# A four-layer decoder on one Trainium2 core: where the slots' zeros are kept, the order of the norm's spreads, an early trial maximum on GpSimd, and one block for convolution and token layouts

## The chip, the cores and the metric

The kernel runs on one core of one Trainium2 chip. The metric is the device time of one execution in microseconds (us); lower is better. Inside the core TensorE (PE; its weight loads are listed as PEld), VectorE (DVE), ScalarE (ACT), GpSimd (POOL) and SyncE (SP) each run their own list of instructions and meet only at semaphores. DMAs here are issued by SP or POOL.

## What is computed

Eight sequences of 256 tokens with 128 features (2048 tokens, held feature by token) pass through four layers, each with self attention, cross attention and a feed-forward part, and each part adds its output to the residual. Every part begins with the first function below; the parts that the change touches inside are the second (layer 1's attention: convolution, SiLU, unit-length heads) and the third (layer 2's feed-forward: the activations are rounded by one scale taken over the whole tensor).

```python
def _layernorm(x, axis=-1, eps=1e-05):
    m = jnp.mean(x, axis=axis, keepdims=True)
    v = jnp.var(x, axis=axis, keepdims=True)
    return (x - m) / jnp.sqrt(v + eps)

# layer 1, attention
q = _causal_depthwise_conv_silu(hidden_states @ q_w, conv_q_w)   # 4 taps; k and v alike
beta = jax.nn.sigmoid(hidden_states @ b_w)
q = _l2norm(q)        # per head of 16 features; k alike
...                   # a delta rule over chunks of 32 tokens
# layer 2, feed-forward
def _act_fake_quant(x, clip_factor):
    scale = jax.nn.sigmoid(clip_factor) * jnp.max(jnp.abs(x)) / QMAX
    return jnp.clip(_ste_round(x / scale), -QMAX - 1.0, QMAX) * scale
```

## The kernel before

The program is a row of blocks. A block gives each engine its own list; at its end all engines meet at a barrier, and the next block's first instructions come after it. `loads_done` is a block of its own, in which only SP waits for a DMA's semaphore, so it holds back everything written after it. Within a block each engine runs its list in the order in which it is written; nothing is reordered.

**The start.** `start_loads` issues the input, the small weights, the context and the masks. `clear_buffers` fills 2560 words of a part of `tiles` (`c.T`, four tiles of 2048 words) with zeros on POOL and has SP copy them to the DRAM buffer `slots_in`, which the experts of layer 0 use later; the zeros lie in tiles 2 and 3. `layer0_attention` issues its weights (`pack_load`), waits with `loads_done` for that copy, and calls `norm_stage`, whose output `n2` is tile 3.

**`norm_stage`** works on 4 chunks of 512 tokens, or 8 parts of 256. PE subtracts the mean (line 270) and sums squares (277), ACT takes squares and roots (398, 407), DVE inverts the roots of two chunks at a time (337). PE then spreads the inverses over the partitions, four parts per inverse (`spreads`, line 290), and DVE multiplies (346). Where `jobs` are handed on, PE multiplies each chunk by the next weights (`follow`, line 314), and ACT or DVE takes the product away. The PE list reads

```python
            spreads(0)
            follow(0)
            spreads(1)
            for i in range(1, NC):
                follow(i)
```

Eight calls have jobs: one with one (the output of layer 2's attention), four with two, two with three and one with four. In the other calls `follow` does nothing.

**Layer 1's convolution and token layouts** are two blocks. `conv_stage` has DVE convolve k, v and q (one multiply and three multiply-adds of 2048 words each, lines 2142 and 2144), ACT apply SiLU in eleven pieces that also permute the tokens (2162) and square k and q (2166), and PE form the gate logits (2131). `delta_tokens` then has PE sum the squares per head (2192, 32 matmuls of 8 columns with the squares as weights), ACT take roots (2207), PE transpose k and v to token rows (2201, eight groups of four), and ACT and DVE copy the groups by turns (2211, 2236). `delta_solve` follows, beginning with PE transposes of the copied keys (2298) that ACT copies.

**Layer 2's feed-forward** (`layer2_mlp`): after the norm, DVE takes the largest magnitude per partition (3450), POOL the largest over the partitions (`partition_all_reduce`, 3421), DVE derives the scale (3453) and rounds (3457, 3458), ACT shifts (3398), PE multiplies (3359). In PE's list 16 products of weights (`join`, 3339) stand ahead of the first of these.

Of the kernel before, what the change touches and what calls it, by code (L numbers as in the profile page):

```python
# [14 lines left out]
P = 128  # L15
# [192 lines left out]
def norm_stage(c, src, dst, eps, centre=True, gain=None, shift=None, times=None, grow=1.0, before=None, add=None,  # L208
# [49 lines left out]
    with nc.Block() as block:  # L258
        @block.tensor
        def _(pe):  # L260
# [64 lines left out]
            follow(0)  # L325
            spreads(1)
            for i in range(1, NC):
                follow(i)
# [669 lines left out]
def clear_buffers(c):  # L998
# [3 lines left out]
    zeros = c.T[:, 2:4, :].rearrange("p a x -> p (a x)")[:, 0:words]  # L1002
# [29 lines left out]
def layer0_attention(c):  # L1032
# [5 lines left out]
    n2 = c.T[:, 3, :]  # L1038
    loads_done(c, c.slots_cleared)
    norm_stage(c, c.X, n2, "eps55", grow=1.0 + 1e-5, also=(c.HN, "eps5"))  # L1040
# [1065 lines left out]
def conv_stage(c, tensors, taps):  # L2106

    nc = c.nc
    a = Arena(c)
    acc = [a.take(N) for _ in tensors]  # L2110
    squares = a.take(2, N)
    ps_g = c.psum[:, 7, 0:2 * P].rearrange("p (n e) -> p n e", e=16)

    def blocks(x):
        return x.rearrange("p (g j t r s) -> p g j t r s", j=4, t=2, r=4, s=32)

    def moves(j):
        if j == 0:
            return [(0, 0, 4)]
        if j == 2:  # L2120
            return [(0, 2, 2), (2, 0, 2)]
        return [(r, r ^ j, 1) for r in range(4)]

    with nc.Block() as block:
        @block.tensor
        def _(pe):
            for n in range(NT):
                b, t = n // 2, n % 2
                for r in range(4):
                    lo = b * S + t * P + 32 * (r ^ (b % 4))  # L2130
                    mm = nc.tensor.matmul(ps_g[32 * r:32 * r + 32, n, :], c.HN[:, lo:lo + 32], c.w("L1a_gates"),
                                          start=True, stop=True, tile_position=(0, 32 * r))
            mm.then_inc(c.gate_logits.sem, 1)

        @block.vector
        def _(dve):
            chain = Chain(dve, c.vector_chain)
            for x, w, y in zip(tensors, taps, acc):
                K = w.shape[1]
                xs = x.rearrange("p (b s) -> p b s", s=S)  # L2140
                ys = y.rearrange("p (b s) -> p b s", s=S)
                chain.link(nc.vector.tensor_scalar(y, x, w[:, K - 1:K], None, ALU.mult))
                for back in range(1, K):
                    ins = nc.vector.scalar_tensor_tensor(ys[:, :, back:], xs[:, :, 0:S - back],
                                                         w[:, K - 1 - back:K - back], ys[:, :, back:],
                                                         ALU.mult, ALU.add)
                    if back < K - 1:
                        chain.link(ins)
                ins.then_inc(c.convolved.sem, 1)
            dve.wait_ge(c.convolved.sem, c.convolved.at(len(tensors)))  # L2150
            chain.clear()

        @block.scalar
        def _(act):
            for n, (x, y) in enumerate(zip(tensors, acc)):
                act.wait_ge(c.convolved.sem, c.convolved.at(n + 1))
                for j in range(4):
                    for lo, at, count in moves(j):
                        w = slice(0, 32 * count)
                        src = blocks(y)[:, :, j, :, lo:lo + count, :].rearrange("p g t r s -> p g t (r s)")  # L2160
                        dst = blocks(x)[:, :, j, :, at:at + count, :].rearrange("p g t r s -> p g t (r s)")
                        ins = nc.scalar.activation(dst[:, :, :, w], src[:, :, :, w], ACT.Silu)
# [2259 lines left out]
```

## Time and profile before

| | |
|---|---|
| time, median of 3 runs | 2698.5 us (2695.79 to 2700.4) |
| the profiled execution's own time | 2686.84 us |
| its span | 2685.0 us |
| busy: PE, DVE, ACT, POOL | 72%, 65%, 43%, 27% |
| instructions | 35915 |

A timeline row gives start, duration, engine, line, operation, output<-input, and in brackets how long the engine stood idle before it and what ended that. Rows of PE merge instructions of one kind; a float32 matmul stands as two instructions in the trace (x64 for 32 matmuls), while a float32 transpose stands as one. A slice of the page is 67 us long.

### The profile page before, as it was taken

The numbers are of one execution on the slowest core, as the hardware profiler recorded it, in microseconds if no ns is written. First come the engines' busy times: TensorE is split into PE (matmuls) and PEld (weight loads), VectorE is DVE, ScalarE is ACT, GpSimd is POOL, SyncE is SP. The second block draws the span as 40 slices with busy tenths as digits, with TensorE's granted clock in tenths as the row PEclk, the third lists the DMA queues.
The fourth block names the chain that finished last, engine by engine and source line by source line (L and its number), as shares of the span: only waits on it lengthen the run. The fifth ranks groups of instructions, "written<-read, shape, count | busy, mean of one in ns | idle before, by whom it ended". The sixth has DMA issues, their size and how long they took to land. (4 is left out here: it accounts for less than half of the span.)

```text
span 2685.0 us, 35915 instructions
## 1 busy us (share of the span) xinstructions
PE 1923.9 (72%) x11203; PEld 1116.0 (42%) x11215; DVE 1756.1 (65%) x5569; ACT 1148.4 (43%) x3148; POOL 716.3 (27%) x638
## 2 busy tenths in 40 slices
PE   5996878843877999979986875556555555556777
PEld 1644436422444666644352543333333333324243
DVE  4235322248766666647746567999999999964554
ACT  3553332141314666641233554555555455542312
POOL 1200050405333333310032411333333333331130
PEclk7988889965988999979988887566666566666878
DMA  4000001220000000000100000000000000000000
GB/s 183 2 1 0 25 19 35 47 110 1 2 2 1 1 1 0 0 0 0 77 14 1 1 1 0 1 1 1 1 1 1 0 1 1 1 1 0 0 0 16
DMA packets 10065, 37.04 MB, mean 14 GB/s; under 512 B 1755, under 2 KB 7008, under 8 KB 8752
## 3 DMA queue, kind: packets, MB, share of 16 engines
q1 hardware_dynamic: 7856, 31.69, 3.0%
q0 software_dynamic: 2048, 3.38, 0.6%
q8 instruction: 80, 1.31, 0.2%
q14 instruction: 81, 0.66, 0.1%
HBM read 30.11 MB, written 5.77 MB: 13 GB/s over the span
## 5 line engine op out<-in xcount | busy, mean ns | idle before, releaser
L3552 PE MATMUL psum<-work 32*128 32x256 f32 x512 | 129.9, 652 | 296.8 <-ACT work L3647 296.8
L3699 DVE MATCH_REPLACE8 work<-work 128x256 f32<-128x256 f32 x768 | 306.4, 414 | 0.0
L3747 POOL TENSOR_TENSOR work<-work 128x1024 f32<-128x1024 f32 x64 | 150.7, 2355 | 509.0 <-ACT work L3647 509.0
L3696 DVE MAX8 work<-work 128x8 f32<-128x256 f32 x768 | 267.8, 415 | 0.0
L3552 PEld LDWEIGHTS psum<-work 32*128 32x128 f32 x512 | 77.3, 309 | 323.1 <-ACT work L3647 165.1
L676 POOL TENSOR_TENSOR work<-work 128x256 f32<-128x256 f32 (+2 forms) x144 | 133.3, 944 | 259.3 <-DVE work L936 259.3
L866 ACT ACTIVATE work<-work 128x128 f32<-128x128 f32 (+1 forms) x320 | 144.9, 454 | 38.0 <-PE psum L736 24.6
L337 DVE RECIPROCAL work<-work 128x256 f32<-128x256 f32 x36 | 62.8, 1749 | 123.2 <-ACT work L407 123.0
L3647 ACT ACTIVATE work<-work 128x256 f32<-128x256 f32 x256 | 128.2, 501 | 0.0
L3575 PE MATMUL psum<-work,tiles 128*8 128x256 f32 x512 | 117.0, 610 | 13.8 <-ACT work L3656 13.8
L3749 POOL TENSOR_TENSOR work<-work 128x1024 f32<-128x1024 f32 x64 | 121.1, 1892 | 6.2 <-DVE work L3721 1.2
L3598 PE MATMUL psum<-small_weights,work 128*128 128x128 f32 x512 | 102.7, 367 | 21.6 <-POOL work L3749 21.6
L3645 ACT ACTIVATE work<-psum,work 128x256 f32<-128x256 f32 x256 | 117.5, 459 | 0.0
L3598 PEld LDWEIGHTS psum<-small_weights,work 128*128 128x128 f32 x512 | 84.3, 194 | 70.1 <-POOL work L3749 52.6
L3699 DVE MATCH_REPLACE8 work<-work,psum 128x256 f32<-128x256 f32 x256 | 103.4, 420 | 0.0
L905 DVE CUSTOM_DVE_ANT_0 work<-psum,work 128x128 f32<-128x128 f32 (+1 forms) x320 | 99.6, 368 | 2.8
L3696 DVE MAX8 work<-psum 128x8 f32<-128x256 f32 x256 | 90.9, 421 | 7.2 <-PE psum L3552 5.8
L2080 DVE TENSOR_TENSOR work<-work,psum 128x320 f32<-128x320 f32 (+1 forms) x56 | 32.1, 574 | 88.4 <-PE psum L1951 88.4
L832 ACT ACTIVATE work<-psum,big_weights 128x256 f32<-128x256 f32 x128 | 57.8, 474 | 73.2 <-PE psum L722 72.8
L796 PE MATMUL psum<-work 128*64 128x256 f32 (+2 forms) x640 | 72.7, 346 | 19.6 <-DVE work L931 19.6
L736 PE MATMUL psum<-small_weights,work 128*128 128x128 f32 x512 | 83.5, 281 | 3.7 <-POOL work L676 3.7
L270 PE MATMUL psum<-residual,small_weights 128*128 128x512 f32 x96 | 58.5, 741 | 38.7 <-PEq L189 22.8
(597 smaller groups left out, 4682.0 us busy)
## 6 DMA issues: line engine op xcount, KB each, us to landing
big_weights<-L0f_dram SPq DMA_DIRECT2D x1, 6053.5 KB, 25.8
big_weights<-L_dram SPq DMA_DIRECT2D x1, 5892.0 KB, 16.6
big_weights<-L_dram SPq DMA_DIRECT2D x1, 4952.5 KB, 15.7
big_weights<-L_dram SPq DMA_DIRECT2D x1, 2091.0 KB, 20.2
big_weights<-L_dram SPq DMA_DIRECT2D x1, 1630.5 KB, 11.8
big_weights<-L0f_dram SPq DMA_DIRECT2D x1, 1630.5 KB, 6.4
slots_in<-tiles SPq DMA_DIRECT2D x1, 1280.0 KB, 9.4
residual<-x_dram SPq DMA_DIRECT2D x1, 1024.0 KB, 4.9
```

The lines of the kernel that those rows point to most:

```text
L676: ins = nc.gpsimd.tensor_tensor(part, part, rsum[:, g % 4, q:U:U // n].unsqueeze(2) .broadcast_to([P, n, seen(q)]), ALU.mult)
L866: ins = nc.scalar.activation(probs[:, g % 2, u, 0:seen(u)], src, ACT.Exp, bias=nbias[:, g % 2, u:u + 1], scale=scale, accum_out=sums[:, g ...
L905: ins = nc.vector.tensor_tensor_reduce(raw[:, s, u, 0:seen(u)], scores(g)[:, u, 0:seen(u)], mask(mb, u % 2)[:, 0:seen(u)], 1.0, NEG, ALU.a ...
L3552: mm = nc.tensor.matmul(scores(n)[:, u, :], qb[head, tile % 2, u % 2 * P:(u % 2 + 1) * P], kb[head, tile % 2, :], start=True, stop=True, t ...
L3575: mm = nc.tensor.matmul(held(tile)[at:at + D, :], values[:, 2 * b + kt, lo:lo + D], turned[:, n % 2, head, kt, :], start=(kt == 0), stop=( ...
L3598: mm = nc.tensor.transpose(bank(4 + head)[:, at:at + P], probs[:, n % 2, 2 * head + q, kt * P:(kt + 1) * P], ident)
L3645: nc.scalar.activation(probs[:, s, u, :], scores(n)[:, u, :], ACT.Exp, bias=nbias[:, s, u:u + 1], scale=SCALE)
L3647: ins = nc.scalar.activation(rest[:, s, u, :], raw[:, s, u, :], ACT.Exp, bias=nbias[:, s, u:u + 1], scale=SCALE)
L3696: ch.step(v.max(top8[:, n % 2, u, r, :], src[:, u, :]))
L3699: ins = v.match_replace(raw[:, n % 2, u, :], top8[:, n % 2, u, r, :], src[:, u, :], REPLACED)
L3747: ch.link(g.tensor_tensor(mine, mine, rest[:, n % 2], ALU.subtract))
L3749: g.tensor_tensor(mine, mine, rsum[:, n % 2, :].unsqueeze(2).broadcast_to([P, U, S]), ALU.mult) \
```

## The change

Four edits.

1. The zeros are kept in tiles 1 and 2, and the block that waits for their copy to DRAM stands behind the first norm instead of ahead of it.
2. In every norm the second half's spreads stand ahead of the first chunk's handed-on products.
3. `conv_stage` and `delta_tokens` become one block, `conv_tokens`. The order is q, k, v; the head sums of q are made after its squares, those of k after its squares; ACT copies six groups and DVE two; ACT loads its function tables five times rather than three.
4. In the norm ahead of layer 2's feed-forward POOL makes a `partition_all_reduce` of a zeroed word.

```diff
@@ norm_stage
             powers(1)
             spreads(0)
-            follow(0)
             spreads(1)
-            for i in range(1, NC):
+            for i in range(NC):
                 follow(i)
@@ clear_buffers
-    zeros = c.T[:, 2:4, :].rearrange("p a x -> p (a x)")[:, 0:words]
+    zeros = c.T[:, 1:3, :].rearrange("p a x -> p (a x)")[:, 0:words]
@@ layer0_attention
     n2 = c.T[:, 3, :]
+    norm_stage(c, c.X, n2, "eps55", grow=1.0 + 1e-5, also=(c.HN, "eps5"))
     loads_done(c, c.slots_cleared)
-    norm_stage(c, c.X, n2, "eps55", grow=1.0 + 1e-5, also=(c.HN, "eps5"))
     loads_done(c, c.big_loaded)
@@ conv_tokens, in place of conv_stage and delta_tokens: PE's list
...
+            mm.then_inc(c.gate_logits.sem, 1)
+            add_heads(0, ps_q)
+            pe.wait_ge(c.permuted.sem, c.permuted.at(2))
+            for n in range(4):
+                turn(n)
+            pe.wait_ge(c.gates_shifted.sem, c.gates_shifted.at(1))
+            add_heads(1, ps_k)
+            pe.wait_ge(c.permuted.sem, c.permuted.at(3))
+            for n in range(4, 8):
+                turn(n)
@@ DVE's list
+            convolve(0)
+            dve.wait_ge(c.gate_logits.sem, c.gate_logits.at(1))
+            chain.link(vec.tensor_tensor(gates, ps_g, mix_b, ALU.add))
+            vec.tensor_tensor(gates, gates, mix_bias, ALU.add).then_inc(c.gates_shifted.sem, 1)
+            convolve(1)
+            convolve(2)
+            dve.wait_ge(c.rooted.sem, c.rooted.at(1))
+            chain.link(vec.reciprocal(inv, lengths))
...
+            for n in by_vector:
+                _, dst, t, b0 = groups[n]
+                dve.wait_ge(c.tokens_turned.sem, c.tokens_turned.at(n + 1))
+                vec.tensor_copy(dst[:, t, b0:b0 + 4, :], bank(n)).then_inc(c.tokens_kept_v.sem, 1)
@@ ACT's list
+            soften(0)
+            square(0)
+            act.wait_ge(c.gates_shifted.sem, c.gates_shifted.at(1))
+            nc.scalar.activation(gates, gates, ACT.Sigmoid).then_inc(c.gates_ready.sem, 1)
+            nc.scalar.activation(warm, c.w("one"), ACT.Silu)
+            soften(1)
+            square(1)
+            for n in range(4):
+                keep(n)
+            act.wait_ge(c.lengths_ready.sem, c.lengths_ready.at(2))
+            nc.scalar.activation(lengths[:, P:2 * P], c.psum[:, 6, 0:P], ACT.Sqrt, bias=c.w("eps12"))
+            nc.scalar.activation(lengths[:, 0:P], c.psum[:, 7, 2 * P:3 * P], ACT.Sqrt, bias=c.w("eps12")) \
+                .then_inc(c.rooted.sem, 1)
+            nc.scalar.activation(warm, c.w("one"), ACT.Silu)
+            soften(2)
+            for n in (4, 6):
+                keep(n)
@@ layer2_mlp
-    norm_stage(c, c.X, c.HN, "eps5")
+    a = Arena(c)
+    a.off = 2 * N
+    trial = a.take(2)
+
+    def first_reduction(pool):
+        nc.gpsimd.memset(trial, 0.0).then_inc(c.zeros_made.sem, 1)
+        pool.wait_ge(c.zeros_made.sem, c.zeros_made.at(1))
+        nc.gpsimd.partition_all_reduce(trial[:, 1:2], trial[:, 0:1], P, bass.bass_isa.ReduceOp.max)
+
+    norm_stage(c, c.X, c.HN, "eps5", beside=(("gpsimd", first_reduction),))
```

`by_vector` is (5, 7); `soften` is the SiLU of one tensor, `square` its squares, `keep` the copy of one group, `turn` a group's four transposes, `add_heads` 16 head sums.

The first place is PE's list at layer 1's norm and what follows it. Before (290 is `spreads`, 314 `follow`, 2131 the gate logits, 2192 the head sums, 2201 the transposes):

```order
L290 MATMUL psum<-work,small_weights 128x256 x4
L314 MATMUL psum<-normed_input,big_weights 128x512 x3
L290 MATMUL psum<-work,small_weights 128x256 x4
L314 MATMUL psum<-normed_input,big_weights 128x512 x9
L258 UNCONDITIONAL_BRANCH
L2125 UNCONDITIONAL_BRANCH
L2131 MATMUL psum<-big_weights,normed_input 32x16 x64
L2124 UNCONDITIONAL_BRANCH
L2187 UNCONDITIONAL_BRANCH
L2192 MATMUL psum<-big_weights,work 128x8 x32
L2201 MATMUL psum<-small_weights,tiles 128x128 x32
```

And now, with the same steps at lines 290, 2773, 2756 and 2766:

```order
L290 MATMUL psum<-work,small_weights 128x256 x8
L314 MATMUL psum<-normed_input,big_weights 128x512 x12
L258 UNCONDITIONAL_BRANCH
L2750 UNCONDITIONAL_BRANCH
L2773 MATMUL psum<-big_weights,normed_input 32x16 x64
L2756 MATMUL psum<-big_weights,work 128x8 x16
L2766 MATMUL psum<-small_weights,tiles 128x128 x16
L2756 MATMUL psum<-big_weights,work 128x8 x16
L2766 MATMUL psum<-small_weights,tiles 128x128 x16
```

The four late spreads moved ahead of the first three products, the block boundary between logits and head sums is gone, and each half of the head sums stands ahead of half of the transposes.

The second place is ACT's list after k's SiLU in the joined block (2835 SiLU, 2840 squares, 2845 copies, 2857 and 2858 roots, 2860 a one-word SiLU, with the semaphore that a row waits for in brackets):

```order
L2840 ACTIVATE work<-tiles 128x2048 [waits permuted]
L2845 COPY work<-psum 128x512 [waits tokens_turned] x4
L2857 ACT_TABLE_LOAD
L2857 ACTIVATE work<-psum,small_weights 128x128 [waits lengths_ready]
L2858 ACTIVATE work<-psum,small_weights 128x128
L2860 ACT_TABLE_LOAD
L2860 ACTIVATE work<-small_weights 128x1
L2835 ACTIVATE tiles<-work 128x2x256 [waits convolved]
```

Before, all three SiLUs and both squares stood ahead of the first root; now v's SiLU stands behind the roots, which wait for the head sums.

The third place is POOL's list at layer 2's feed-forward, first before (3419 clears a buffer, the row without operands at 3421 belongs to the reduction behind it):

```order
L449 UNCONDITIONAL_BRANCH
L3417 UNCONDITIONAL_BRANCH
L3419 MEMSET work 128x768
L3421 ISA
L3421 ISA work<-work 128x1
L3427 COPY work<-big_weights 128x8x4
```

and now (3331 and 3333 are the trial in the norm's block, 3443 and 3445 the old steps):

```order
L3331 MEMSET work 128x2
L3333 ISA
L3333 ISA work<-work 128x1
L258 UNCONDITIONAL_BRANCH
L3441 UNCONDITIONAL_BRANCH
L3443 MEMSET work 128x768
L3445 ISA work<-work 128x1
L3451 COPY work<-big_weights 128x8x4
```

The row without operands moved with the first reduction into the norm's block; the real reduction has none of its own any more.

## Rows read from the trace of the kernel before

**Rows 1.** Page, part 2: TensorE's granted clock in 40 slices, tenths of full.

```profile
PEclk7988889965988999979988887566666566666878
```

**Rows 2.** Waits of SP's queue, 0 to 40 us: total, times, longest.

```profile
SPq L189 <- DMA slots_in<-tiles: 6.3, 1, 6.3
```

**Rows 3.** Timeline, 0 to 75 us: start, duration, engine, line, operation.

```profile
8.13 0.64 SPq L174 DMA_DIRECT2D big_weights<-L0f_dram  x1
...
15.83 4.34 PE L270 MATMUL psum<-residual,small_weights 128*128 128x512 f32 x6 [15.83 <-PEq L189]
...
31.20 2.81 DVE L352 SCALAR_TENSOR_TENSOR normed_input<-normed_input,psum 128x256 f32<-128x256 f32 x8
...
34.70 0.23 DVE L1231 COPY work<-big_weights 128x128 f32<-128x128 f32 x1 [0.69 <-PEq L189]
```

**Rows 4.** DMA issues, 0 to 40 us: KB, us from issue to landing.

```profile
big_weights<-L_dram SPq DMA_DIRECT2D x1, 1630.5 KB, 11.8
slots_in<-tiles SPq DMA_DIRECT2D x1, 1280.0 KB, 9.4
```

**Rows 5.** Line 290 in eight windows, one per late spread: length, PE busy, clock.

```profile
554.30:555.30 1.00, 0.91 (x8) 0.74 0.00 0
...
sum 8.30, PE 7.59; mean PE 0.95
```

**Rows 6.** Line 346 (DVE): what its engine sat idle for, us, times.

```profile
  PE psum L290: 37.7, 8
```

**Rows 7.** Timeline, layer 1's norm.

```profile
547.74 1.75 DVE L337 RECIPROCAL work<-work 128x256 f32<-128x256 f32 x1 [0.58 <-ACT work L407]
...
550.14 4.28 PE L314 MATMUL psum<-normed_input,big_weights 128*128 128x512 f32 x6 [1.22 <-DVE normed_input L346]
```

**Rows 8.** Timeline, layer 1's convolution and token layouts.

```profile
565.46 7.08 DVE L2144 SCALAR_TENSOR_TENSOR work<-tiles,big_weights,work 128x2040 f32<-128x2040 f32 x3
...
572.57 2.84 ACT L2162 ACTIVATE tiles<-work 128x512 f32<-128x512 f32 x11 [7.19 <-DVE work L2144]
...
591.92 3.69 ACT L2166 ACTIVATE work<-tiles 128x2048 f32<-128x2048 f32 x2
...
595.91 13.79 PE L2192 MATMUL psum<-big_weights,work 128*128 128x8 f32 x64 [30.52 <-PEq L2124]
...
611.29 1.28 ACT L2214 ACT_TABLE_LOAD   x1
612.58 0.42 ACT L2214 ACTIVATE work<-work 128x256 f32<-128x256 f32 x1
...
613.95 2.48 DVE L2236 COPY work<-psum 128x512 f32<-128x512 f32 x4
...
616.75 2.04 PE L2298 MATMUL psum<-small_weights,work 128*128 128x128 f32 x16 [1.40 <-PEq L2186]
```

**Rows 9.** Windows: length, PE, PEld, DVE, ACT, POOL busy, clock.

```profile
577.00:595.90 18.90, 0.00 (x0) 0.02 (x1) 12.01 (x6) 9.30 (x25) 0.00 (x0) 0.50 0.00 0
595.90:609.50 13.60, 13.59 (x64) 13.60 (x65) 0.85 (x2) 1.25 (x1) 0.00 (x0) 0.50 0.00 1
609.50:612.50 3.00, 3.00 (x15) 3.00 (x16) 1.75 (x1) 2.27 (x3) 0.00 (x0) 0.50 0.00 0
613.00:620.00 7.00, 5.30 (x46) 4.86 (x45) 4.58 (x9) 3.70 (x7) 0.39 (x1) 1.00 0.00 1
```

**Rows 10.** Timeline, layer 2's feed-forward.

```profile
1580.73 2.29 DVE L3450 TENSOR_REDUCE work<-normed_input 128x1 f32<-128x2048 f32 x1 [0.32 <-PEq L258]
...
1581.94 5.56 PE L3339 MATMUL psum<-big_weights 128*128 128x128 f32 x32
...
1587.24 0.38 POOL L3421 PARTITION_ALL_REDUCE work<-work  x1 [5.81 <-issue]
...
1587.65 0.16 DVE L3453 TENSOR_TENSOR work<-work,big_weights 128x1 f32<-128x1 f32 x1 [4.64 <-POOL work L3421]
...
1590.33 0.38 PE L3359 MATMUL psum<-work 128*128 128x512 bf16 x1 [2.83 <-ACT work L3398]
```

More of the change, by code:

```diff
@@ L2102, in layer0_experts @@
         s.advance(n)
[L2106 to L2162, printed above, removed]
-                ins.then_inc(c.permuted.sem, 1)
-            for n, x in enumerate((tensors[0], tensors[2])):
-                act.wait_ge(c.permuted.sem, c.permuted.at((1, 3)[n]))
-                nc.scalar.activation(squares[:, n, :], x, ACT.Square)
-    c.gate_logits.advance(1)
-    c.convolved.advance(len(tensors))
-    c.permuted.advance(len(tensors))
-    return squares
@@ L2865, in layer1_attention @@
     norm_stage(c, c.X, c.HN, "eps5", jobs=[(c.w(f"L1a_w{s}"), None, None, t, None) for s, t in zip("qkv", (q, k, v))])
-    squares = conv_stage(c, [k, v, q], [c.w(f"L1a_conv_{s}") for s in "kvq"])
     def words(lo, *dims):
@@ L2891, in layer1_attention @@
     probs = [c.T[:, 3, 0:12 * P].rearrange("p (j a x) -> p j a x", a=3, x=P), words(at, 4, 3, P)]
-    delta_tokens(c, k, v, squares, kt, vt, gates, lengths, inv, sizes)
+    conv_tokens(c, q, k, v, [c.w(f"L1a_conv_{s}") for s in "qkv"], kt, vt, gates, lengths, inv, sizes)
     delta_solve(c, kt, vt, sizes, sizes_r, k_r, X, tri, pair, own)
@@ L3311, in layer2_mlp @@
     loads_done(c, c.loaded_ahead)
-    norm_stage(c, c.X, c.HN, "eps5")
+    a = Arena(c)
+    a.off = 2 * N
[5 more added lines that the diff above has]
+    norm_stage(c, c.X, c.HN, "eps5", beside=(("gpsimd", first_reduction),))
+    c.zeros_made.advance(1)
     a = Arena(c)
```

159 lines of the change are left out of this document (96 added, 63 removed).

## The prediction

> **What bounds the kernel now.** I first read the page's clock line: TensorE is granted full clock only in part, down to 5 and 6 tenths in the second half [rows 1]. No engine is busy all the time, so a local edit is worth what it takes off the wait that ends last at its place. I therefore went from the waits to the timeline of four places. At the start everything stands behind the copy of zeros to DRAM: SP waits 6.3 us for it [rows 2]. In the norms with handed-on products DVE idles 37.7 us in 8 places for late spreads [rows 6], which themselves hold PE for 7.6 us [rows 5]. In layer 1, PE does nothing from 577 to 595.9 and then 13.8 us of head sums while ACT and DVE wait [rows 8, 9]. In layer 2's feed-forward a reduction that takes 0.4 us starts at 1587.2, though its input is there at 1583.0 [rows 10].
>
> **The start: 6.3 us.** SP has issued the big weights at 8.77 (8.13 + 0.64); the first norm starts at 15.83 [rows 3], because the copy of the zeros lands at 5.97 + 9.4 = 15.4, where 5.97 is its issue [rows 4]. Now the norm starts at about 9.2. It ends 6.3 earlier, at 27.7 instead of 34.0 (31.20 + 2.81) [rows 3]. What is late next: the zeros' copy is down at 15.4, and layer 0's weights, issued just ahead of 8.13, at about 19.6 (11.8 after issue) [rows 4]. Both lie under the norm, so nothing takes the wait's place. The DMA of zeros has the same size and is read from tiles that the norm doesn't write. The bounds are close: 6.0 if one barrier more stands in the way, 6.6 if the whole stretch from 8.77 to 15.4 goes.
>
> **The spreads: 7.0 us.** In eight norms four spreads stand between the first chunk's products and the rest. They take 0.95 us on average, 7.6 in total [rows 5], and behind them PE runs products one after another to the end of the stage, so time taken from there counts. DVE's idle 37.7 us is not the gain: DVE is off the path once its four parts are early, and PE still has the same products. What comes back is a delay at the new place. In layer 1's norm the second reciprocal ends at 549.49 and the first product starts at 550.14 [rows 7]; 0.9 us of spreads now stand in between, so it starts about 0.3 late, and that stage gains 0.6. Four norms are like this, by 0.1 to 0.5. In the other four the first product waits for a further step on ACT or POOL, or for another bank, and the spreads hide. Small gaps around the old place, and one wait for a later chunk, go too (0.6 us, my estimate). So 7.6 - 1.2 + 0.6 = 7.0. The upper bound is 8.5 (no collision and every gap gone). The lower bound is zero: should each early set delay the first product by its whole length, PE has only exchanged the two; below zero is excluded, since the products and their number stay.
>
> **Convolution and layouts: 12.9 us.** All in times of the old trace. DVE is through with the first tensor at 572.5, and each further one takes 8.3 (565.46 + 7.08; ACT's last SiLU starts at 591.92 - 2.84 = 589.1, two tensors later) [rows 8]. New path:
> - SiLU of q 572.6 to 575.4, squares (half of 3.69) to 577.3, 16 head sums on PE: half of 13.79 is 6.9, to 584.2. PE has been idle till then and its clock is at 0.50 [rows 9].
> - DVE adds 0.85 for the gates [rows 9] and is through with k at 581.7. SiLU of k to 584.6, squares to 586.5. Between them on ACT lie the sigmoid and two table loads (0.42 + 2 x 1.28 and a word, 3.2 us), hidden in its wait from 577.3 to 581.7.
> - PE turns k's four groups from 584.6: 15 transposes took 3.0 us at 0.50 [rows 9], so 16 take 3.4, to 588.0. Then k's head sums: 6.9 at that level, to 594.9, or 3.45 at twice the clock, to 591.5.
> - ACT copies four groups meanwhile and loads the root's table under its wait. Queued behind the wait for the head sums on ACT is everything for v: two short roots 0.6 (from 0.42 for a sigmoid of twice the width), table load 1.28 and one word 0.2, SiLU of v 2.84. That is 4.9 us, to 599.8 or 596.4; v itself has been convolved since 590.0. PE's last transposes wait for it: 3.4, one copy on DVE 0.62 (2.48 for four) and hand-overs 0.2; the block's end costs 0.3 (616.43 to 616.75) [rows 8].
>
> So the keys' transposes of the next block start at 604.3 or 600.9 instead of 616.75: 12.4 or 15.8 earlier. There the old trace had clock 1.00 from 613.0 on [rows 9] and 16 transposes in 2.04 [rows 8]. After 5 us without work on PE they may now run at 0.50, 3.4 us, which costs up to 1.4. Bounds: 11.0 and 15.8. I take 12.9, nearer to the low end, as the only row for head sums is at 0.50.
>
> Which end it is hangs on what lifts the clock. The rows show 13.6 us of unbroken head sums at 0.50, and 1.00 from 613.0 on, 3.5 us after the transposes began [rows 9]. That speaks for the transposes lifting it, and with them the second head sums. The Trainium skill (TensorE: Matmul & The Clock Gate, Part 4: PE-mode transpose) says that transposes don't count as PE being busy in the way matmuls do. By that rule k's head sums would stay at 1.2 GHz; the trace leans against it.
>
> One more table load (ACT, behind the roots) is on the path, at 1.28: in the old trace the sigmoid starts 0.01 us after its load ends [rows 8]. The Trainium skill (ScalarE: Activation LUTs, What ACT_TABLE_LOAD costs) states 2.66 us for a switch, drain included. By that the sum would be 1.4 less, an estimate from the page; the trace shows no such drain, and I keep 1.28.
>
> **The trial maximum: 2.8 us.** The old reduction starts 5.8 us after the clearing of a buffer, "issue" being all that it waits for [rows 10], and its row without operands now stands in the norm's block. That block lasts some 10 us on PE and DVE with POOL empty, so 5.8 + 0.4 + a small clearing hide there. The real one can start when DVE's maximum is there (1580.73 + 2.29 = 1583.0), so DVE goes on at 1583.5 instead of 1587.65: 4.1 earlier. But PE has 16 weight products ahead of the first product of the activations, until 1581.94 + 5.56 = 1587.5, and that first product started at 1590.33 [rows 10]. Once ACT's part is 4 us early, PE's own list is late next: 1590.33 - 1587.5 = 2.8. Upper bound 4.1, lower bound 0 (the 5.8 us belong to each block anew).
>
> **Sum.** 6.3 + 7.0 + 12.9 + 2.8 = 29.0. The profiled execution, 2686.84, would become 2657.8. The median of the runs is 11.7 higher, 2698.5; the gain is the same in us, so 2669.5.
>
> **Rivals.**
> - The second head sums stay at 1.2 GHz, and so does the start of the next block. 11.0 instead of 12.9, rounded with the rest: 2671.4. For it: 13.6 us at 0.50 in the only rows of such work. Against: the rise after the transposes.
> - The early spreads cost at the new place what they did at the old. Then 22.0 remain: 2676.5. For it: in four norms DVE's first two parts take only 0.65 us. Against: that covers most of 0.9, and in the other four a further step follows.
> - Upper ends everywhere: 6.6 + 8.5 + 15.8 + 4.1 = 35.0, so 2663.5. For it the clock's rise behind the transposes; against it PE's 16 products.
> - The trial doesn't do what it says: the reduction in the next block waits anew. 26.2 remain: 2672.3. Against it: the second reduction of the old block has no such row ahead of it.
> - Slower: layer 0's experts, slices 5 to 8 of the page, some 230 us at 8 to 9 tenths of the clock [rows 1] with PE the busy engine. They now begin some 8 us earlier against the start. Should the clock stay at the lower level there for t us more than before, it costs t/2; from 58 us on that eats the 29 us, and with 70 the time is 2704.5. Against it: the list there is unchanged, and the clock falls where PE stands idle.
> - Nothing of it arrives, as the stages hide one another: within 0.2% of 2698.5. Against it: barriers at every block.
>
> **How the numbers follow.** Forecast 50%, the second head sums at 1.2 GHz 20, spreads without gain 10, upper ends 10, trial in vain 5, slower 3, nothing 2. So faster 95, same 2, slower 3; "same" is within 0.2% (5.4 us), what a measurement of this kernel can tell from no change. The lower bounds together, 6.0 + 0 + 11.0 + 0 = 17.0, give 2681.5, the upper ones 2663.5. With some 2 us of spread between medians I give 2661 to 2682.
>
> **What would show it.** The first norm's matmuls start at about 9.2. Line 346 no longer waits for line 290, and products follow without a break. The head sums are in two runs of about 6.9 and 3.5 to 6.9 us; Layer 1 begins some 8.5 us earlier (6.3 and the norms before it), so v's SiLU starts at 585 to 589 and the next block's transposes of keys at 592 to 596. The reduction starts within 0.2 us of DVE's maximum. It is wrong if the clock at layer 1's head sums is at another level than both cases, if another DMA ends the start, or if an expert stage changes its length by more than 3 us.

## Result and the profile after

| | before | after |
|---|---|---|
| time, median of 4 runs, us | 2699.24 (2695.79 to 2700.4) | 2662.49 (2659.91 to 2665.62) |
| the profiled execution's own time | 2686.84 | 2659.91 |
| its span | 2685.0 | 2658.1 |
| ratio | | 0.9866 [0.9849, 0.9884] |

36.8 us less, where 29.0 were forecast; 2662.5 lies in the given range, near its lower end. The profiled executions are only 26.9 us apart. I cut both spans at the first root of each of the 18 norms (the one-word root on ACT with which a norm begins):

| stretch (between first roots) | before | after | gain |
|---|---|---|---|
| up to the first norm | 17.09 | 10.64 | 6.5 |
| layer 0 up to its experts | 290.0 | 289.5 | 0.6 |
| layer 0's experts | 232.6 | 242.3 | -9.7 |
| layer 1's first norm and attention | 293.0 | 278.4 | 14.6 |
| the rest of layer 1 | 499.1 | 499.5 | -0.5 |
| layer 2's attention | 89.2 | 85.2 | 4.0 |
| norms and cross attention of layer 2 | 150.0 | 145.4 | 4.6 |
| layer 2's feed-forward | 54.6 | 51.8 | 2.8 |
| the rest | 1059.4 | 1055.3 | 4.1 |

TensorE's granted clock on the page, for [rows 1]: it is low in the same parts.

```profile
PEclk7988889875988999989997896566666566667878
```

Each edit shows at its place. The start, in after's timeline, and the next stage behind the norm, for [rows 3]:

```profile
9.38 4.78 PE L270 MATMUL psum<-residual,small_weights 128*128 128x512 f32 x6 [9.38 <-PEq L170]
...
25.18 2.80 DVE L351 SCALAR_TENSOR_TENSOR normed_input<-normed_input,psum 128x256 f32<-128x256 f32 x8
29.06 0.23 DVE L1230 COPY work<-big_weights 128x128 f32<-128x128 f32 x1 [1.07 <-PEq L189]
```

The norm begins 6.45 earlier (15.83 in [rows 3]), and SP's wait of [rows 2] is gone. The boundary behind the norm takes 1.07 instead of 0.69: the block that waits for the zeros' copy stands there now. The next stage's first copy on DVE starts at 29.06 instead of 34.70, only 5.6 earlier: 0.4 went to that boundary and 0.4 to the norm's first centring products, which took 4.78 instead of 4.34.

The norms: what DVE's multiplication (line 345, formerly 346) and PE's handed-on products (314) cost and wait for in the whole program (busy us, mean ns, then the idle time ahead of them). First before, then after.

```profile
L314 PE MATMUL psum<-normed_input,big_weights 128*128 128x512 f32 x96 | 50.9, 676 | 8.5 <-ACT normed_input L412 4.4 <-DVE normed_input L346 4.1
L290 PE MATMUL psum<-work,small_weights 32*128 32x256 f32 x288 | 42.2, 462 | 15.1 <-DVE work L337 9.6 <-ACT normed_input L403 5.2
L314 PE MATMUL psum<-tiles,big_weights 128*128 128x512 f32 x48 | 29.4, 767 | 6.3 <-POOL tiles L458 2.6 <-ACT tiles L412 2.3 <-DVE tiles L346 1.5
```

```profile
L314 PE MATMUL psum<-normed_input,big_weights 128*128 128x512 f32 x96 | 50.4, 681 | 0.7 <-ACT normed_input L411 0.7
L290 PE MATMUL psum<-work,small_weights 32*128 32x256 f32 x288 | 46.2, 484 | 18.7 <-DVE work L336 13.2 <-ACT normed_input L402 5.3
L314 PE MATMUL psum<-tiles,big_weights 128*128 128x512 f32 x48 | 27.6, 741 | 0.8 <-POOL tiles L457 0.8
...
L345 DVE SCALAR_TENSOR_TENSOR normed_input<-normed_input,psum 128x256 f32<-128x256 f32 x120 | 40.2, 406 | 0.1
```

DVE's 37.7 us of waiting for spreads [rows 6] are gone. PE stood 8.5 + 6.3 = 14.8 us ahead of its products before, and 1.5 after; the spreads wait 18.7 us instead of 15.1. Where these 14.8 us lie decides what they mean. The timeline of before has 14.5 of them ahead of the very first product of the eight norms (2.57, 2.07, 1.22, 1.50, 2.26, 1.98, 1.22 and 1.64), and 0.34 in one place behind it. One such norm, of layer 2, before and then after:

```profile
1443.58 0.71 PE L290 MATMUL psum<-work,small_weights 32*128 32x256 f32 x8 [1.47 <-DVE work L337]
1446.55 3.78 PE L314 MATMUL psum<-tiles,big_weights 128*128 128x512 f32 x4 [2.26 <-ACT tiles L412]
1450.26 1.24 PE L290 MATMUL psum<-work,small_weights 32*128 32x256 f32 x8
1451.43 5.94 PE L314 MATMUL psum<-tiles,big_weights 128*128 128x512 f32 x12
```

```profile
1427.62 1.24 PE L290 MATMUL psum<-work,small_weights 32*128 32x256 f32 x8 [0.59 <-DVE work L336]
1429.39 1.50 PE L290 MATMUL psum<-work,small_weights 32*128 32x256 f32 x8 [0.54 <-DVE work L336]
1430.82 8.34 PE L314 MATMUL psum<-tiles,big_weights 128*128 128x512 f32 x16
```

The first product comes 3.20 us after the first spreads instead of 2.97, so the filled wait itself brings nothing; the gain lies between the first and the last product. Over the eight norms the first products come 2.2 us later behind the first spreads, and the stretch from first to last product is 9.7 us shorter (90.7 to 81.0).

Layer 1's convolution and layouts in after's timeline, for [rows 8]:

```profile
578.95 6.99 PE L2756 MATMUL psum<-big_weights,work 128*128 128x8 f32 x32 [12.01 <-ACT work L2840]
...
586.11 3.67 PE L2766 MATMUL psum<-small_weights,tiles 128*128 128x128 f32 x16 [0.17 <-ACT tiles L2835]
...
589.58 3.93 PE L2756 MATMUL psum<-big_weights,work 128*128 128x8 f32 x32
...
593.82 0.36 ACT L2858 ACTIVATE work<-psum,small_weights 128x128 f32<-128x128 f32 x1
594.19 1.28 ACT L2860 ACT_TABLE_LOAD   x1
...
595.49 0.20 ACT L2860 ACTIVATE work<-small_weights 128x1 f32<-128x1 f32 x1
595.60 2.82 ACT L2835 ACTIVATE tiles<-work 128x512 f32<-128x512 f32 x11
...
603.20 3.65 PE L2160 MATMUL psum<-small_weights,work 128*128 128x128 f32 x16 [1.05 <-PEq L2749]
```

From DVE's first step of the convolution (564.13 before, 565.68 after) to the next block's transposes (616.75 before [rows 8]) 52.6 us passed, now 37.5. Those transposes take 3.65 us instead of 2.04.

The feed-forward of layer 2 in after's timeline, for [rows 10]: first the trial, then the real maximum.

```profile
1555.46 0.38 POOL L3333 PARTITION_ALL_REDUCE work<-work  x1 [5.69 <-issue]
...
1560.68 2.29 DVE L3474 TENSOR_REDUCE work<-normed_input 128x1 f32<-128x2048 f32 x1 [0.32 <-PEq L258]
...
1561.89 5.95 PE L3363 MATMUL psum<-big_weights 128*128 128x128 f32 x32
...
1563.07 0.35 POOL L3445 PARTITION_ALL_REDUCE work<-work  x1 [1.69 <-DVE work L3474]
...
1567.89 0.38 PE L3383 MATMUL psum<-work 128*128 128x512 bf16 x1
```

The trial takes the 5.7 us of "issue", the real reduction starts 0.1 us behind the end of DVE's maximum, and PE goes over to the activations when its products of weights end at 1567.8.

What doesn't fit are the experts. In after's trace ACT and DVE stand still there for 25.7 and 27.0 us, as in no row of the first trace of before ("remote" is the name that the profile gives to what ended the wait):

```profile
514.87 0.60 ACT L1980 ACTIVATE work<-psum 128x512 f32<-128x512 f32 x1 [25.72 <-remote]
```

```profile
517.72 1.42 DVE L2079 TENSOR_TENSOR work<-work,psum 128x512 f32<-128x512 f32 x2 [26.98 <-remote]
```

### The profile page after: what moved, and what is told of

Its sections match the earlier page's. It is cut to its first block and busy times, and to the rows that moved or that the text cites. A ratio compares the mean times of both kernels' runs of the same rounds, so it can differ in the third digit from the quotient of the medians.

```text
span 2658.1 us, 35910 instructions
## 1 busy us (share of the span) xinstructions
PE 1915.9 (72%) x11203; PEld 1113.3 (42%) x11215; DVE 1755.9 (66%) x5567; ACT 1152.6 (43%) x3155; POOL 716.7 (27%) x640
## 5 line engine op out<-in xcount | busy, mean ns | idle before, releaser
L1980 ACT ACTIVATE work<-psum 128x512 f32<-128x512 f32 (+1 forms) x64 | 33.1, 517 | 133.3 <-PE psum L1949 92.0
```

## Experiments

Two theories stood against each other on the missing 10 us (theory A: a stall that comes and goes, whichever kernel runs; theory B: one that the change makes). Beside that each edit was run alone, so that its term of the sum has a measured size. Gains in us are one minus the ratio, times the median of before on that chip. (By the medians alone the four edits give 4.4, 11.0, 14.4 and 4.7 us, all within the intervals below.) Three chips took part beside the first occasion: A (the first four runs, before at 2683.3), B (the next four, 2686.3) and C (the last three, 2697.1).

### Before again (chip A)

No edit.

> The kernel before, unchanged, once more with a profile. The question is the expert stage (its last product of experts to the next norm's first root), which took 9.7 us less in the first profile of before than in the one of after. Theory A (a stall that most executions have): ACT and DVE stand still for about 25 us while GpSimd issues the 32 gathers, PE idles some 20 us, the tail behind the last gather is about 22 us and the stage some 10 us longer than in the first profile; the execution is near the median, 2696 to 2700, and the first profile of before was the exception. Theory B (the change itself makes the stall): no such stall here, the tail behind the gather is 8.4 us again, and the execution is at about 2687 or its extra time lies elsewhere.

2684.53 us, its expert stage 230.4 us, no stall. So this run alone does not back theory A; before itself is 16 us quicker here (2683.3) than on the first occasion (2699.2).

### Each edit alone (chips A and B)

The start:

```diff
-    zeros = c.T[:, 2:4, :].rearrange("p a x -> p (a x)")[:, 0:words]
+    zeros = c.T[:, 1:3, :].rearrange("p a x -> p (a x)")[:, 0:words]
-    loads_done(c, c.slots_cleared)
     norm_stage(c, c.X, n2, "eps55", grow=1.0 + 1e-5, also=(c.HN, "eps5"))
+    loads_done(c, c.slots_cleared)
```

> Only the first edit: the slots' zeros in tiles 1 and 2, and the wait for their copy behind the first norm. By the prediction 6.3 us less than before (ratio 0.9977), the first norm starting at about 10.6 instead of 17.1. Rival: part of it is lost because one more block boundary now stands between the norm and the attention (about 1 us) and since PE meets its first work colder: 5 to 5.6 us in all. If the expert stage's stall hangs on where in time the stage begins, this kernel's expert stage differs from before's by some 10 us in either direction.

Ratio 0.9982 [0.9973, 0.9991]: 4.8 us (2.4 to 7.2). The first root is at 10.51 instead of 16.73, so 6.2 at the place; the expert stage is as in before (231.9). The interval holds the forecast and the rival. The traces speak for less than 6.3: DVE's first copy of the next stage starts at 34.4 to 35.3 in the six traces without this edit and at 28.6 to 29.8 in the six with it as it stands here, 5.8 earlier on average. The added boundary (1.07 instead of 0.69) is 0.4 of what is missing.

The spreads:

```diff
             spreads(0)
-            follow(0)
             spreads(1)
-            for i in range(1, NC):
+            for i in range(NC):
                 follow(i)
```

> Only the second edit: in every norm with handed-on products all eight spreads stand ahead of the products. By the prediction 7.0 us less (ratio 0.9974), between 0 and 8.5. From the traces of before and after the norms and what follows them, clock included, suggest 6 to 12. Rival: the early spreads only swap places with the first products, so under 2 us. In the profile DVE's multiplications have no idle time left for the spreads if the first is right.

Ratio 0.9952 [0.9938, 0.9965]: 12.9 us (9.4 to 16.6), above my upper bound of 8.5. The rows of lines 314 and 290 in this kernel:

```profile
L314 PE MATMUL psum<-normed_input,big_weights 128*128 128x512 f32 x96 | 48.5, 659 | 0.3 <-ACT normed_input L411 0.3
L290 PE MATMUL psum<-work,small_weights 32*128 32x256 f32 x288 | 46.1, 483 | 19.3 <-DVE work L336 13.8 <-ACT normed_input L402 5.2
L314 PE MATMUL psum<-tiles,big_weights 128*128 128x512 f32 x48 | 28.0, 748 | 0.8 <-POOL tiles L457 0.8
```

The wait ahead of the products falls from 14.8 to 1.1, that ahead of the spreads rises by 4.2. As in after, nearly all of what falls stood ahead of the first products, where the early spreads now fill it. So these two sums are no measure of the gain. The eight norms, cut in three, are (before again and before are traces of the kernel before; sums in us; before again and the edit alone ran on one chip):

| stretch | before again | before | after | spreads alone |
|---|---|---|---|---|
| norm's first root to its first spread | 55.2 | 56.6 | 57.0 | 52.9 |
| first spread to first product | 26.3 | 26.2 | 28.4 | 29.4 |
| first to last product | 92.5 | 90.7 | 81.0 | 79.5 |
| together | 173.9 | 173.6 | 166.4 | 161.7 |

Alone, the edit makes the eight norms 12.2 us shorter, near the timed 12.9; in after they are 7.2 shorter than in before. The difference lies mostly in the first row, in the centring ahead of the spreads, which no edit touches, and there the granted clock differs: in one norm of layer 3 it is 0.92 with the edit alone, 0.79 in before and 0.78 in after, and the stretch takes 9.3, 10.9 and 11.0 us. The trace of this kernel is its slowest run, and only 7.8 us shorter than before again: the eight stages that begin with these norms are 14.6 us shorter, but stages without an edit took longer (2.3 us in the experts, 3.7 in the rest of layer 1, 1.3 in layer 2's feed-forward).

The convolution:

```diff
-    squares = conv_stage(c, [k, v, q], [c.w(f"L1a_conv_{s}") for s in "kvq"])
-    delta_tokens(c, k, v, squares, kt, vt, gates, lengths, inv, sizes)
+    conv_tokens(c, q, k, v, [c.w(f"L1a_conv_{s}") for s in "qkv"], kt, vt, gates, lengths, inv, sizes)
```

> Only the third edit: convolution and token layouts in one block. By the prediction 12.9 us less (ratio 0.9952). From the trace of after the sharper value is 15.1 for the block and 1.6 lost in the transposes behind it, so 13.5. Rival: layer 2's attention, which was 4 us shorter in after without an edit of its own but the spreads, owes that to this edit (the clock's level handed on): then 16 to 18.

Ratio 0.9938 [0.9925, 0.9952]: 16.6 us (12.9 to 20.1), where the rival had put it. In its trace layer 1's first norm and attention take 271.2 us against 289.9 in before again. Of these 18.7 us 15.4 are the block (52.7 to 37.3); the other 3.3 come from the rest of the attention, transposes of the next block included, which has no edit and takes 210 to 218 us in the traces with the joined block and 214 to 216 in the others. And layer 2's attention takes 85.2 against 89.2. That 4 us goes with TensorE's clock, 0.92 against 0.88 on the stage's average. PE stands idle ahead of that stage's norm in both; in before again the clock falls to 0.50 in that pause, here it stays at 1.00. The first centring products, and windows with the clock (third number from the end), of before again and of this kernel:

```profile
1328.23 5.46 PE L270 MATMUL psum<-residual,small_weights 128*128 128x512 f32 x6 [3.54 <-PEq L170]
```

```profile
1328.30:1333.60 5.30, 5.30 (x6) 1.75 (x6) 0.00 (x0) 2.58 (x4) 0.00 (x0) 0.50 1.13 427
```

```profile
1312.43 2.81 PE L270 MATMUL psum<-residual,small_weights 128*128 128x512 f32 x6 [3.65 <-PEq L170]
```

```profile
1308.80:1312.40 3.60, 0.00 (x0) 0.00 (x0) 2.05 (x3) 0.00 (x1) 0.00 (x0) 1.00 0.00 0
1313.00:1315.70 2.70, 2.70 (x14) 0.86 (x12) 0.00 (x0) 2.38 (x5) 0.00 (x0) 1.00 0.66 279
```

The six products take 5.46 and 2.81 us. The pauses are 3.54 and 3.65 us long, and the longer one keeps the clock; so it is in all 13 traces, 3.65 in the six that keep it and 3.54 in the seven that lose it, so that the pause's length is not what decides. All traces with the joined block have 85.2 there, but for the kernel with v's SiLU first below (86.9); all without have 89.1 to 89.4. Why the clock falls in the one and not in the other is open.

The trial maximum:

```diff
-    norm_stage(c, c.X, c.HN, "eps5")
+    a = Arena(c)
+    a.off = 2 * N
+    trial = a.take(2)
+    ...
+    norm_stage(c, c.X, c.HN, "eps5", beside=(("gpsimd", first_reduction),))
+    c.zeros_made.advance(1)
```

> Only the fourth edit: the trial maximum on GpSimd in the norm ahead of layer 2's feed-forward. By the prediction 2.8 us less (ratio 0.9990), between 0 and 4.1, with DVE going on 4 us earlier and PE's 16 products of weights late next. Rival: the 5.8 us belong to each block anew, then 0, and the real reduction again starts 4 us behind DVE's maximum. The timed interval will hardly tell 2.8 from 0; the profile's rows will.

Ratio 0.9987 [0.9977, 0.9996]: 3.5 us (1.1 to 6.2). The stage takes 51.5 us instead of 54.3 to 54.6 in the three traces of before, that is 2.9 to 3.1 less. The rival falls: the real reduction has no "issue" ahead of it.

```profile
1580.55 0.35 POOL L3431 PARTITION_ALL_REDUCE work<-work  x1 [1.69 <-DVE work L3460]
```

### After again (chip B)

No edit.

> The kernel after, unchanged, beside before on one chip. The single edits gained 4.4, 11.0 and 14.35 us there; with some 2.8 for the trial maximum the sum is 32.5 (ratio 0.988). Theory A (the stall in the expert stage comes and goes from execution to execution or from chip to chip, in before and after alike): in the profile here the products of layer 0's experts run through while GpSimd issues the gathers, the tail behind the last gather is some 8.5 us, and the gap to before is the sum, about 32. Theory B (all four edits together make the stall): PE again idles some 20 us at the gathers, in this kernel alone, and the gap to before is only some 22.

2643.38 us against 2686.26, ratio 0.9840 [0.9826, 0.9853]: 42.9 us. There is no stall, and the expert stage takes 227.5; theory B falls, though the gap is not theory A's 32 either. But the gap is more than the sum of the single edits, 4.8 + 12.9 + 16.6 + 3.5 = 37.8 (the intervals of these terms would allow it), and 46.2 between the spans of this trace and before again. Of these 46.2, 10.5 lie in stretches that no edit touches, and where the mean clock was higher (0.89 against 0.86, 0.87 against 0.85, 0.92 against 0.88): layer 0's attention 156.6 instead of 160.2, the experts 227.5 instead of 230.4, layer 2's attention 85.2 instead of 89.2. The attention of layer 0, before again and after again:

```profile
17.00:177.00 160.00, 139.49 (x1327) 76.96 (x1326) 63.19 (x131) 83.87 (x99) 23.00 (x13) 0.86 0.10 42
```

```profile
11.00:167.00 156.00, 135.96 (x1327) 75.23 (x1326) 63.19 (x131) 83.59 (x98) 23.24 (x13) 0.89 0.15 60
```

### Head sums ahead of the transposes (chip B)

```diff
             add_heads(0, ps_q)
-            pe.wait_ge(c.permuted.sem, c.permuted.at(2))
-            for n in range(4):
-                turn(n)
             pe.wait_ge(c.gates_shifted.sem, c.gates_shifted.at(1))
             add_heads(1, ps_k)
+            pe.wait_ge(c.permuted.sem, c.permuted.at(2))
+            for n in range(4):
+                turn(n)
```

> After, with the head sums of k ahead of the transposes of k on PE. A question on the clock, not a better kernel. Theory A (the transposes lift the clock): q's and k's head sums both run at 0.50, 7.0 us for 16 each, as the 32 in before did, and the clock rises only some 3.5 to 4 us after the first transpose; the block is some 6 us longer, since ACT's copies of k's groups, and behind them the roots and v's SiLU, wait for the later transposes. Theory B (the clock would have risen at that point whatever PE did, after so much work of any kind): it rises within k's head sums, about 11 us after q's began, and they take 4 to 6 us; the block is some 4 us longer.

Windows of this kernel (clock third from the end): q's sums, k's sums, k's transposes, the next block's transposes, behind them.

```profile
567.00:574.00 7.00, 6.93 (x32) 6.83 (x32) 6.93 (x4) 5.88 (x15) 0.00 (x0) 0.50 0.00 0
576.20:583.00 6.80, 6.80 (x33) 6.80 (x34) 3.24 (x2) 0.00 (x0) 0.00 (x0) 0.50 0.01 2
583.00:586.50 3.50, 3.50 (x17) 3.21 (x17) 0.00 (x0) 1.76 (x3) 0.00 (x0) 0.50 0.00 0
598.20:601.00 2.80, 2.80 (x14) 2.80 (x15) 0.91 (x1) 1.17 (x2) 0.00 (x0) 0.50 0.00 0
602.00:604.00 2.00, 1.21 (x11) 1.02 (x10) 1.70 (x2) 0.27 (x1) 1.65 (x1) 1.00 0.00 0
```

The time was 2649.91 us; from q's sums to the next block's transposes it takes 31.2 us (566.94 to 598.18) against 24.3 in after, 7 more. Theory B falls: both runs of head sums stay at 0.50, 14 us of them. Theory A holds in that the clock rises only behind transposes, and not in its time. It had the rise 3.5 to 4 us after the first transpose; k's transposes (583.0 to 586.6) and v's (593.5 to 597.1) ran at 0.50 to their end, and the clock rose at about 601, within the next block's, which began at 598.18. So transposes aren't sure to bring it. In after it is at 1.00 some 5 us after k's transposes began, and back at 0.50 at 594; in after again k's sums ran at 0.50 throughout. After, then after again:

```profile
586.10:589.60 3.50, 3.49 (x17) 3.49 (x18) 3.43 (x3) 3.45 (x4) 0.00 (x0) 0.50 0.02 5
591.00:593.00 2.00, 2.00 (x20) 2.00 (x19) 0.49 (x1) 0.71 (x1) 0.00 (x0) 1.00 0.00 0
```

```profile
571.00:577.60 6.60, 6.60 (x33) 6.60 (x31) 1.78 (x1) 1.87 (x2) 0.00 (x0) 0.50 0.00 1
```

Of the six traces in which k's transposes stand ahead of k's sums, five have sums of 3.8 to 4.1 us and one 6.8. In the one, after again, the block takes 40.2 us instead of 37.5, but the next block's transposes then meet a clock of 1.00 and take 2.05: 12.4 us gained in all, where after's quick sums gave 13.5.

### v's SiLU ahead of the roots (chip B)

```diff
+            soften(2)
             act.wait_ge(c.lengths_ready.sem, c.lengths_ready.at(2))
             ...
-            nc.scalar.activation(warm, c.w("one"), ACT.Silu)
-            soften(2)
-            for n in (4, 6):
+            for n in (4, 5, 6):
                 keep(n)
```

> After, with v's SiLU ahead of the two roots on ACT (v is convolved 4.1 us before ACT comes to it), one table load less, and three of v's groups copied by ACT, one by DVE. In after DVE's last copy ended 7.3 us behind the start of v's SiLU. Now v's SiLU starts at once after k's copies (4.1 us earlier), and the path behind it goes over the table load, two roots, the reciprocal, three small operations and one copy on DVE: 1.28 + 0.74 + 1.75 + 0.7 + 0.7 = 5.2 after the SiLU's 2.84. So the block ends some 3 us earlier than in after, 2.5 to 4 with the clock of v's transposes; against after a ratio of about 0.9989. Rival: the reciprocal, later by the SiLU, becomes the bound and only the table load is gained, 1.3 us.

2639.96 us, 3.4 below after again by medians; ratio to before 0.9830 [0.9816, 0.9843], which overlaps after's. At the place, from k's transposes to those of the next block:

```profile
569.43 3.47 PE L2766 MATMUL psum<-small_weights,tiles 128*128 128x128 f32 x16 [0.17 <-ACT tiles L2835]
...
583.30 3.35 PE L2160 MATMUL psum<-small_weights,work 128*128 128x128 f32 x16 [1.89 <-PEq L2749]
```

13.9 us, where after took 603.20 - 586.11 = 17.1, with head sums as quick as here (3.9): 3.2 gained. The rival (1.3) falls.

### A third occasion (chip C)

No edit to either kernel.

> The kernel before, a third profile, for the expert stage. Seven of the eight traces since the first one of after show no stall of ACT and DVE at the gathers, and before ran at 2683 and 2686 us on those occasions against 2699 on the first. Theory A (the stall belongs to some chips or occasions): before is at about 2684 here and its expert stage takes 230 to 233 us, or it is near 2699, and then ACT and DVE stand still some 25 us at the gathers. Theory B (before never has it): near 2699 without such a stall.

2699.91 us, and the stall is there, in before. (The text says seven of eight traces; it was eight of eight.) The last gather, and ACT's and DVE's rows around it:

```profile
523.56 0.60 ACT L1981 ACTIVATE work<-psum 128x512 f32<-128x512 f32 x1 [23.27 <-remote]
523.72 1.00 POOL L1854 DMA_INDIRECT tiles<-slots_out,tiles  x1 [0.30 <-issue]
527.10 0.69 DVE L2080 TENSOR_TENSOR work<-work,psum 128x512 f32<-128x512 f32 x1 [25.22 <-remote]
527.84 0.50 PEld L1950 LDWEIGHTS psum<-normed_input,big_weights 128*128 128x128 f32 x2 [20.42 <-issue]
```

The expert stage takes 246.4 us instead of 230.4. ACT and DVE go on as GpSimd issues the last of its gathers.

> The kernel after, a third time, beside before. The ratio was 0.9866 [0.9849, 0.9884] on the first occasion and 0.9840 [0.9826, 0.9853] on the second. If the gain is the same on every occasion it is about 0.985 here. In the profile k's head sums take 3.9 us if the clock rises behind k's transposes, as in four of five traces with this order, or 6.9 us if it does not, as in the second trace of after.

2659.44 against 2697.06, ratio 0.9857 [0.9842, 0.9872]: 38.6 us. The stall is there too, and its expert stage takes 244.0:

```profile
516.38 0.60 ACT L1980 ACTIVATE work<-psum 128x512 f32<-128x512 f32 x1 [22.54 <-remote]
```

The intervals of the three occasions overlap. The stall adds to both kernels alike: the expert stage is 16.0 us longer than in before again and 16.5 longer than in after again. k's head sums took 3.8 us. (The text counts four of five traces with the quick sums; up to then it was three of four.)

### The better version (chip C)

```diff
+            soften(2)
             ...
-    loads_done(c, c.slots_cleared)
-    loads_done(c, c.big_loaded)
+    loads_done(c, c.slots_cleared, c.big_loaded)
```

> The kernel with v's SiLU ahead of the roots, and the two waits at the start (the zeros' copy, the weights) in one block instead of two. Against after: some 3.0 us from the SiLU's place, as in v_first (3.4 there, by medians), and 0.4 from one block boundary less (1.07 us between the norm and the attention in after, 0.69 in before). So a ratio to after of 0.9987, near 0.9837 to before if after is at 0.985. Rival: the clock's level in the blocks behind moves by as much as that, and the two kernels can't be told apart.

This is v's SiLU first, as above, and one block for the two waits at the start. 2651.53 us, 7.9 below after by medians; ratio to before 0.9838 [0.9824, 0.9851] against 0.9857 [0.9842, 0.9872], intervals that just overlap. From k's transposes to the next block's it is 13.9 again, against 16.9 in after on this chip. In the two traces the expert stage differs as well (238.2 instead of 244.0), which no edit touches. Moving the SiLU is faster than after on both chips by medians, and by 3.1 to 3.2 at the place; of the one boundary less the trace shows 0.76 us where after has 1.07, which the times can't tell.

## Why the prediction came out as it did

**The sign, the order of size, the range and each place were right.** Term by term:

- Start, 6.3: 6.2 to 6.5 at the norm's first root, but 5.8 on average at the next stage, just below my bound of 6.0, and 4.8 (2.4 to 7.2) timed. The barrier that I had as a bound is there (1.07 instead of 0.69), and it is most of what is missing.
- Trial maximum, 2.8: 2.8 to 3.1 at the place. PE's 16 products of weights were late next, as worked out.
- Convolution, 12.9: the block became 15.1 shorter and the next transposes 1.6 longer (3.65 less 2.04), 13.5 together; timed 16.6 (12.9 to 20.1), as layer 2's attention then also met a higher clock (4.0). The steps stand (in after two runs of head sums, 7.0 and 3.9 us, the second starting before the clock has risen; v waits on ACT behind the roots). I had put the levels as two fixed cases, 11.0 and 15.8, and took a value between them. The runs showed both levels of the second head sums, the higher one five times of six, and they are nearer to each other than I had them, 13.5 and 12.4, since the quick sums went with slow transposes behind and the slow ones with quick transposes. That 12.9 lies between is in part luck.
- Spreads, 7.0: the mechanism was right. The products behind the first one did run one after another before (0.34 us of waiting in all eight norms), so taking the late spreads out of their row counts in full, and the first products wait for a further step in four norms and are late in the other four. The sizes were a little off: from first to last product 9.7 less where 7.6 + 0.6 was forecast, the first products late by 2.2 instead of 1.2 (0.3, 0.8, 0.2 and 0.8, where I had 0.1 to 0.5 each), so 7.5 net, and 7.2 with the centring ahead of it. Alone the edit gave 12.9 (9.4 to 16.6), above the upper bound of 8.5. What that bound left out is the clock: of the 12.2 us by which the eight norms are shorter in that trace, 2.3 lie in the centring ahead of the spreads, and the products' own time fell by 5.5 (82.0 to 76.5) while that of the spreads rose by 4.1 (42.0 to 46.1). The term put the clock at nothing in both directions, and no run tells how much of the 12.9 would come again.

**What the forecast put at nothing** is the clock's level outside these places. In the first pair of traces the four places give 5.6 + 7.2 + 13.5 + 2.8 = 29.1, where 29.0 were forecast. The spans without the expert stage are 36.6 us apart, near the timed 36.8. So 7.5 us lie in stretches without an edit: 4.0 in layer 2's attention, where the clock is shown, 1.7 behind the last root, and about a microsecond each in two stages behind a norm that was edited. The forecast missed 36.8 by 7.8, and this is nearly all of it.

On the rival "second head sums at 1.2 GHz": it is one of the two cases that occur, not a wrong one; one execution in six had it. The Trainium skill (TensorE: Matmul & The Clock Gate, Part 4: PE-mode transpose) says that transposes don't count as PE being busy as matmuls do. The runs here disagree: with the head sums first, PE ran nothing but transposes from 583.0 to the rise at 601, the last of them from 598.18, and 14 us of matmuls of 8 columns ahead of them left the clock at 0.50. ACT's table load behind the roots cost 1.28 and 0.02 us of gap (594.19 to 595.49), as the rows of before had it; the 2.66 of the Trainium skill (ScalarE: Activation LUTs, What ACT_TABLE_LOAD costs) did not show.

**The falsifier on the expert stage struck**, -9.7 us, and its cause is not the change. It is a stall that before shows as well, on the occasion on which its time was again near 2699. In all, four traces have it (after, and the three of chip C), nine have not. It also moved what the forecast gives as times: v's SiLU at 595.6 and the next block's transposes at 603.2 are 585.9 and 593.5 without the 9.7 us, both as forecast. The first trace of before is one of those without; its time, 2686.84, is near that of before on chips A and B (2683.3, 2686.3), while its timed runs (2698.5) were like those of chip C (2697.1). So the 11.7 us between the profiled execution and the median, which I carried over unexplained, are near the size of this stall (246.4 less 232.6, the stage in the third and the first trace of before, is 13.8). That those timed runs had it is inferred from their times, not seen. Carrying it over in us was right, as it fell on both kernels.

## What to carry to other kernels

When a row says that an engine stood idle for 14.8 us ahead of its products, look in the timeline which product it stood ahead of: here it was the first of each norm, and work moved into that wait brings the first product no earlier. The gain is what the work held up at its old place. Compare an edit's place with the same place in several traces before you name a cause: stages without an edit moved by 4 us and more from trace to trace here. When a profiled execution and the timed median differ by more than the spread of the runs, find the stage before you build on either: profile the unchanged kernel again on another occasion. And where work stands on one engine in the order in which it was thought of (roots, then the SiLU of a tensor ready 4 us before), ask what the engine could do during the wait.

## What the hardware showed that was not expected

- ACT and DVE stand still together for 19 to 27 us ("remote") while GpSimd issues 32 indirect DMAs of 1.0 us each 1.3 us apart, and go on about when the last is issued (523.56 and 527.10 with the last at 523.72). The expert stage takes 238 to 246 us with it and 227 to 233 without. It was in the first trace of after and in all three of chip C, but not in the first trace of before nor in any of the eight of chips A and B, whichever kernel ran. The cause was not tested.
- TensorE's clock went up 2.9 to 4.4 us after k's transposes began in five traces of six, not in the sixth, and it did not go up in 14 us of matmuls with 8 columns. After it had risen it fell to 0.50 again within such matmuls (convolution alone: up at 587.2, down at 590.5, the sums end at 591.4).
- A pause of 3.65 us on PE kept the clock at 1.00 and one of 3.54 us lost it; the next norm's products took twice as long (5.46 and 2.81 us). Layer 2's attention is 4 us longer with the clock lost, without any edit there. Layer 0's attention (3.6 us) and the experts (2.9) also moved with the mean clock; what made it differ there was not looked into.
